# A four-layer graph network on one core: the second layer's adjacency product moves from VectorE to GpSimd, ahead of the transposes

## The reference

```
A (layer 0): e_ij = x_i.a_i + x_j.a_j, normalised over the graph, times adj plus adj, leaky relu,
             softmax over i, alpha @ x, sigmoid
B+C (layer 1): h = x Wp + bp; scores = leaky(s_src_i + s_dst_j) where adj > 0; attn = softmax over j
             weighted_adj = attn * adj;  h_gat = relu(layernorm(weighted_adj @ h))
             h_gin = (1+eps) h_gat + adj @ h_gat; z = relu(layernorm(h_gin W1 + b1)); relu(z W2 + b2 + h_gat)
D (layer 2): softmaxed adjacency (the same for all graphs), split in diagonal and rest: two products
E (layer 3): h = x W; attn = softmax(leaky(src_i + dst_j)) on edges and loops; elu(attn @ h)
```

## Time and profile before

| | us |
|---|---|
| median of 3 runs (1245.16 to 1245.55) | 1245.51 |
| the profiled execution's own time | 1249.84 |
| its span, first to last instruction | 1248.1 |
| busy: PE, DVE, ACT, POOL | 1111.1, 1096.2, 1020.0, 449.1 |
| share of the span | 89%, 88%, 82%, 36% |

### The profile page before, as it was taken

One profiled execution on the slowest core, in us unless ns is written; L12 is line 12 of the kernel. 1 busy time (PEld: TensorE's weight loads), 2 busy tenths in 40 slices (PEclk: granted clock), 3 DMA queues, 4 the chain that ended last, 5 costly groups with the idle time before them and its releaser, 6 DMA issues.

```text
span 1248.1 us, 29006 instructions
## 1 busy us (share of the span) xinstructions
PE 1111.1 (89%) x7632; PEld 903.1 (72%) x7632; DVE 1096.2 (88%) x4212; ACT 1020.0 (82%) x2582; POOL 449.1 (36%) x832
## 2 busy tenths in 40 slices
PE   6447889999999999999999999999999999999863
PEld 3235677888777777778877777777888777778753
DVE  5656789999999999999999999999999999998743
ACT  2244679999999888998999988889999999889764
POOL 4002324343334343444333334434443334443320
PEclk9667999999999999999999999999999999999986
DMA  3000001101100111111011011111101100110000
GB/s 64 17 26 9 27 26 35 35 26 34 34 22 20 34 34 34 34 34 34 25 34 33 10 32 34 34 34 34 34 25 34 34 21 21 34 35 26 18 9 17
DMA packets 59460, 35.94 MB, mean 29 GB/s; under 512 B 3873, under 2 KB 54817, under 8 KB 59425
## 3 DMA queue, kind: packets, MB, share of 16 engines
q1 hardware_dynamic: 59424, 35.54, 9.4%
HBM read 18.75 MB, written 8.39 MB: 22 GB/s over the span
## 4 chain that ended last, share of the span: by engine, by line
DVE 37%; PE 21%; issue 20%; POOL 9%; ACT 5%; DVEq 2%; DMA 1%; POOLq 0%; ACTq 0%; SPq 0%
PE ps L792 5%; DVE pTB L954 4%; DVE wE L928 3%; PE ps L761 3%; PE ps L777 3%; DVE vA L1027 3%; PE ps L667 3%; DVE wE L941 2%; DVE vA L1046 2%; POOL lnr_E L593 2%; POOL lnr_B L593 2%; DVE wB L928 2%; PE ps L660 2%; ACT xout L1213 2%; DVE wB L941 2%
## 5 line engine op out<-in xcount | busy, mean ns | idle before, releaser
L777 PE MATMUL ps<-hE,pTE 128*128 128x128 f32 x1024 | 136.4, 277 | 0.0
L708 PE MATMUL ps<-xsA,pA 128*128 128x128 f32 x1024 | 124.0, 280 | 7.4 <-ACT xsA L1268 7.4
L777 PE MATMUL ps<-hB,pTB 128*128 128x128 f32 x1024 | 126.3, 277 | 0.0
L777 PEld LDWEIGHTS ps<-hE,pTE 128*128 128x128 f32 x1024 | 125.0, 193 | 0.6 <-issue 0.4
L708 PEld LDWEIGHTS ps<-xsA,pA 128*128 128x128 f32 x1024 | 118.5, 194 | 9.2 <-ACT xsA L1268 8.3
L792 PE MATMUL ps<-gin_j,hgat 128*128 128x512 f32 x256 | 123.7, 607 | 0.0
L826 PE MATMUL ps<-att_j,xD 128*128 128x512 f32 x256 | 122.8, 603 | 0.0
L777 PEld LDWEIGHTS ps<-hB,pTB 128*128 128x128 f32 x1024 | 120.9, 194 | 0.1
L1258 ACT ACTIVATE pA<-vA,nmA,rirA 128x512 f32<-128x512 f32 x128 | 103.6, 816 | 16.7 <-issue 15.6
L928 DVE SCALAR_TENSOR_TENSOR wE<-ps,hE,y2E 128x512 f32<-128x512 f32 x128 | 94.7, 745 | 25.2 <-ACT y2E L1290 23.7
L1027 DVE CUSTOM_DVE_ANT_0 vA<-ps,adj_j 128x512 f32<-128x512 f32 x128 | 84.8, 682 | 17.7 <-PE ps L695 13.6
(11 more groups left out here) (237 smaller groups left out, 3115.2 us busy)
## 6 DMA issues: line engine op xcount, KB each, us to landing
xA<-in_x_dram SPq DMA_DIRECT2D x32, 256.0 KB, 2.8
xrA<-in_x_dram SPq DMA_DIRECT2D x32, 256.0 KB, 2.6
xrB<-xB SPq DMA_DIRECT2D x32, 256.0 KB, 2.3
out_dram<-xout SPq DMA_DIRECT2D x32, 256.0 KB, 2.2
adj_i<-in_adj_dram SPq DMA_DIRECT2D x1, 1024.0 KB, 5.3
a<-in_L_gnn_a_dram SPq DMA_DIRECT2D x2, 64.0 KB, 4.7
w_sb<-in_L_gnn_W_dram SPq DMA_DIRECT2D x2, 64.0 KB, 3.9
l2w<-in_L_gnn_W_dram SPq DMA_DIRECT2D x2, 64.0 KB, 3.4
```

What stands on the lines that cost most here:

```text
L708: last = mm(at("aggA")[:, i * P:(i + 1) * P], pA[:, j, i * P:(i + 1) * P], xsA[:, j], start=(j == 0), stop=(j == NT - 1))
L777: last = mm(at("agg" + n)[:, i * P:(i + 1) * P], att[n]["pT"][:, i, j], att[n]["h"][:, j, 0:P], start=(j == 0), stop=(j == NT - 1))
```

## The change

mult_B moves to GpSimd and ahead of the transposes: it multiplies the weights, as they come from the exponential, with adj_i (not transposed). PE transposes the product, and ScalarE copies the transposed tiles to pT, as it does for E. The exponential of B now writes into w in place, and the buffer that was p holds the product (paB). Beside that the steps' order on all five engines, the number of graphs by which each step lags, and the table of banks are written anew. No other step computes anything else than before. In the diff the first mult_B is the new one in GpSimd's program, the second the old one in VectorE's; the changed waits belong to weights_T (pT_B) and to leaky (L_B0).

```diff
+        paB = att[B]["p"]
+        att[B]["p"] = att[B]["w"]
         IN_BANK = [
-            [("aggA", 2), ("pairA0", 1), ("pE0", 5), ("aggE", 5)],
+            [("h012B", 2), ("h012E", 5), ("pairA2", 1), ("pB3", 2), ("aggA", 1), ("sumA", 0)],
...
+            def mult_B(i):
+                def step(g):
+                    pool.wait_ge(s["expB"], g.tile(i))
+                    if i == 0:
+                        pool.wait_ge(s["pTB"], NT * g.last)
+                    pool.tensor_tensor(paB[:, i], att[B]["p"][:, i], adj_i[:, i], ALU.mult).then_inc(s["paB"], 1)
...
-                READ_BY[f"pB{j}"] = ("paB", j, NT)
+                READ_BY[f"pB{j}"] = ("pcB", j, NT)
...
-                    pe.wait_ge(s["exp" + n], g.tile(i))
+                    pe.wait_ge(s["paB" if n == "B" else "expE"], g.tile(i))
...
-            agg_B0, agg_B1, agg_B2, agg_B3 = (aggregate("B", i, "paB") for i in range(NT))
+            agg_B0, agg_B1, agg_B2, agg_B3 = (aggregate("B", i, "pcB") for i in range(NT))
...
-                        dve.wait_ge(s["exp" + n], NT * g.last)
+                        dve.wait_ge(s["paB" if n == "B" else "expE"], NT * g.last)
...
-            def mult_B(i):
-                def step(g):
-                    dve.wait_ge(s["pTB"], g.tile(i))
-                    if i == 0:
-                        dve.wait_ge(s["aggB"], NT * g.last)
-                    v.tensor_tensor(att[B]["pT"][:, i], tiles(at(f"pB{i}")), adj_j[:, :, i * P:(i + 1) * P],
-                                    ALU.mult).then_inc(s["paB"], 1)
...
-            def copy_pE(i):
-                    act.wait_ge(s["pTE"], g.tile(i))
+            def copy_p(n, i):
+                    act.wait_ge(s["pT" + n], g.tile(i))
                     if i == 0:
-                        act.wait_ge(s["aggE"], NT * g.last)
-                    a.copy(att[E]["pT"][:, i].rearrange("p t d -> p (t d)"), at(f"pE{i}")).then_inc(s["pcE"], 1)
+                        act.wait_ge(s["agg" + n], NT * g.last)
+                    a.copy(att[n]["pT"][:, i].rearrange("p t d -> p (t d)"), at(f"p{n}{i}")).then_inc(s["pc" + n], 1)
...
-                t.run(mult_B0, 1)
-                t.run(bn_D, 3)
-                t.run(q_C, 2)
-                t.run(join_D, 3)
-                t.run(mult_B1, 1)
```

More of the change, by code:

```diff
@@ L600, in _ @@
             rstd_A, rstd_B, rstd_Z, rstd_C, rstd_D, rstd_E = (rstd(k) for k in "ABZCDE")
+            def mult_B(i):
[4 more added lines that the diff above has]
+                    pool.tensor_tensor(paB[:, i], att[B]["p"][:, i], adj_i[:, i], ALU.mult).then_inc(s["paB"], 1)
+                return step
+            mult_B0, mult_B1, mult_B2, mult_B3 = (mult_B(i) for i in range(NT))
             def power_A(g):
@@ L1177, in turn @@
                 t.run(M_B0, 1)
+                t.run(L_B2, 1)
                 t.run(M_B1, 1)
[L1179 to L1181 removed]
+                t.run(M_B2, 1)
+                t.run(v_A0, 0)
+                t.run(bn_Z, 2)
                 t.run(L_B3, 1)
[L1183 removed]
+                t.run(join_Z, 2)
+                t.run(v_A1, 0)
                 t.run(M_B3, 1)
[L1185 to L1202 removed]
+                t.run(v_A2, 0)
+                t.run(v_A3, 0)
+                t.run(max_A, 0)
+                t.run(lrelu_A0, 0)
+                t.run(offset_A, 0)
+                t.run(lrelu_A1, 0)
+                t.run(lrelu_A2, 0)
+                t.run(L_E0, 4)
+                t.run(L_E1, 4)
+                t.run(lrelu_A3, 0)
+                t.run(M_E0, 4)
+                t.run(M_E1, 4)
+                t.run(zz_B, 1)
+                t.run(recip_A, 0)
+                t.run(L_E2, 4)
+                t.run(M_E2, 4)
+                t.run(q_C, 2)
+                t.run(L_E3, 4)
+                t.run(bn_B, 1)
+                t.run(join_B, 1)
+                t.run(stats_B, 1)
+                t.run(M_E3, 4)
+                t.run(y_C, 2)
+                t.run(y_A, 0)
+                t.run(bn_A, 0)
+                t.run(join_A, 0)
             turns(dve, turn)
@@ L1417, in turn @@
+                t.run(norm_Z, 2)
+                t.run(exp_A0, 0)
+                t.run(exp_A1, 0)
+                t.run(copy_pB2, 1)
+                t.run(copy_zT, 2)
+                t.run(exp_A2, 0)
+                t.run(exp_A3, 0)
+                t.run(copy_pB3, 1)
+                t.run(scale_xA, 0)
                 t.run(norm_E, 5)
+                t.run(copy_xTD, 3)
             turns(act, turn)
```

209 lines of the change are left out of this document (88 added, 121 removed).

## The result

| | before | after |
|---|---|---|
| median of the runs, us | 1245.53 | 1353.41 (1349.13 to 1354.64) |
| ratio, 95% interval | | 1.0835 (1.0803 to 1.0867) |
| profiled execution: own time, span | 1249.84, 1248.1 | 1354.57, 1352.9 |
| first join_A ends, last join_A ends | 77.4, 1140.7 | 76.8, 1234.7 |
| mean period between them (31) | 34.30 | 37.35 |

The change costs 8.3%. Slower was the likelier side of the prediction, but the time lies 68 us above its range.

The account below looks back on a forecast made before the run. A loop of waits through several engines was taken as the bound: 32.9 us plus 1.95 of GpSimd holds gives 34.9 per graph; 178.3 + 31 x 34.9 = 1260.2, less 2.6, plus 1.3: 1259 us, range 1228 to 1285.

Parts of the forecast that it names:

- late load of xA: SyncE's load of the next graph's x: no wait was priced, its data being wanted some 7 us after release.
- steady period without it (31 graphs): Time per graph in the steady part: forecast 34.9 us, from 32.9 plus 1.95 of holds.
- what the filling saves: Between first and last A statistics joins: 31 periods less 6.5 us, taken unchanged from the kernel before.
- emptying: From last join_A to the end: 107.4 us kept, plus 1.3 for one product; up to 10 more possible.
- start: Up to the first graph's join of A statistics: 77.4 us, left as in the kernel before.
- The SP order ... costs nothing: SyncE's queue, both loads at the turn's start, xrB next: claimed free, xA's load released after scale_xA.
- The quarrel: GpSimd products and VectorE's two-SBUF-input steps exclude each other: mult_B2 and mult_B3 delay lrelu_A1 and lrelu_A2, 1.95 us together.
- the loop of 32.9: Aggregate A, VectorE's turn to lrelu_A3, exp_A3, copy_pB3, scale_xA, next aggregate A: 32.9 us, 34.9 with holds.
- the second loop: Shares the first loop's beginning, leaves VectorE at join_Z, then rstd_Z, norm_Z, four exp_A and copies on ScalarE: 34.0 us.
- the rivals: Harmless products, 1231 us, chance 0.24; one meeting, 1237 to 1247, 0.12; full VectorE relief, 1206, 0.05; late ScalarE, 1290, 0.09.
- The last one: ScalarE late with norm_C ahead of y2_B, so L_B0 starts late: with 1 us, period 35.9, median 1290; chance 0.09.
- lrelu_A keeps its 0.67 us: VectorE's lrelu_A unheld would show the forecast wrong; it expected two of four near 1.6 and 1.7 us.

Follow-up runs that it names:

- experiment 1: Changed kernel with only SyncE's order edited: the next graph's load of xA issued ahead of the store and the copy to xrB; 1296.14 us, ratio 1.0371.
- experiment 10: Kernel before with only SyncE's order taken from the changed kernel (load xA, load xrA, copy to xrB, store); 1247.09 us, ratio 0.9986.
- experiment 3: Changed kernel with the load of xA ahead and the GpSimd product cut to 4 of 512 columns, the rest filled by memset; 1242.07 us, ratio 0.9947.
- experiment 2: Changed kernel with the GpSimd product cut to 4 of 512 columns, the rest filled with ones by memset; 1313.41 us, ratio 1.0513.
- experiment 8: Kernel before with four products on GpSimd, each covering only 4 of 512 columns, and four copies on ScalarE; 1317.71 us, ratio 1.0555.
- experiment 9: Kernel before with only tile 3's product moved to GpSimd and its copy to ScalarE behind relu_E; 1257.60 us, ratio 1.0063.
- experiment 7: Kernel before with all four products on GpSimd and copies on ScalarE, other orders, lags and banks as before; 1332.11 us, ratio 1.0667.

## Why the prediction was wrong, point by point

Its formula was span = start + middle + end; with the forecast period and 1.3 us for one product in the last chain it gave 1261.5, and the span was 1352.9. The 91.4 us between are:

| term | forecast | changed kernel | off by | shown by |
|---|---|---|---|---|
| late load of xA | 0 | 57.5 | 57.5 | experiment 1 |
| steady period without it (31 graphs) | 34.9 | 35.4 | 15.5 | experiment 1 |
| what the filling saves | 6.5 saved | 3.0 lost | 9.5 | joins of experiment 1 |
| emptying | 108.7 | 118.2 | 9.5 | joins |
| start | 77.4 | 76.8 | -0.6 | joins |

- **The step that failed** is "The SP order ... costs nothing: the load of xA is released after scale_xA and its data is wanted by dots_A some 7 us later." Both halves were right by themselves. What I left out is what stands in front of the load in SyncE's list, and what that waits for: the copy to xrB, which waits for y_C, which the new VectorE order had put near the turn's end. The distance that I had put at 7 us was 8.0 (from 627.03 to 635.01, when dots_A could have begun). 6.7 us of waiting in the list and 2.9 of transfer don't fit into it, and 1.6 us are left over for dots_A to wait. Experiment 1 takes this wait away and nothing else, and experiment 10 shows that it needs both edits. The 57.5 us contain the long turns, which go with the load; at full clock it is 1.7 us a graph.
- **The quarrel**: size of the holds right, victims wrong, and so their price. I had 1.95 us on the second and third lrelu_A; it was 2.05 on max_A and offset_A. The product began at 617.81, when VectorE had just got to max_A, a step earlier than in my timing. I had let these 128x4 steps pass for free, because they are short. It makes a difference for the price: lrelu_A2 lies late in the order and would have delayed exp_A3 alone, the loop of 32.9; max_A and offset_A lie ahead of every exponential of A, and exp_A0 waits 1.47 us. So the hold came on top of the second loop: 33.8 (experiment 3) and 1.6 give 35.4. The prediction said 34.0 and 0.9.
- **The Trainium skill** (SBUF — State Buffer, "Who interferes with whom") had led me to the steps with two SBUF inputs. It holds for the small steps too: max_A is one, and was held for 1.0 us, and so is stats_B, by 0.6. The page also counts tensor_scalar among the operations that may take the shared ports with one input, and the trace agrees: offset_A was held by the product, and in experiment 2 still for 0.4 us by a fill that only writes, while max_A, which only needs the shared read port by that page, was not (162 ns).
- **The loop of 34.0 over norm_Z and ScalarE** was right (33.8 in experiment 3; the 0.2 us that rstd_Z was to wait for mult_B1 fall away there). Because of it, taking 2.44 us a graph off VectorE gains at best 0.7 of period (34.5 to 33.8), and filling and emptying take two thirds of that back: experiment 3 is only 8 us shorter than the kernel before, by spans.
- **The emptying** "could cost up to 10 us ... or nothing": it cost 10.8. It is 115 to 119 us in all kernels with the new lags and 107 to 111 in those with the old. I had carried none of it in the forecast.
- **Of the rivals** none was near. The last one, 1290 us with L_B0 late, had the right side; its mechanism (y2_B late) doesn't appear among the waits. What I named as a sign against the forecast, "lrelu_A keeps its 0.67 us", did occur.
- **Small slips**: VectorE's 860.4 us over 26 periods are 33.09 a graph and not 33.07, and PE's 856.7 are 32.95. Neither changes a forecast.
- **The range** took in the bounds of the terms that I had doubted, and nothing for the one that I had argued to zero.

Open: why the clock falls after some standstills and not after others; how much of the emptying is due to which lag; and whether an order exists in which the real products cost nothing. The best one that ran with all four products on GpSimd stays 1.7% above the kernel before.

## What to carry to other kernels

Of every transfer that is moved, read the list in front of it: the time at which it leaves is set by the latest wait of any entry ahead of it, and that wait may belong to a step which another part of the same change has moved. When work goes from one engine to a second, put the new instructions on the second engine's line between the two events that the loop goes through (here exp_B3 and scale_xA); if they all lie between, the period pays for them although that engine isn't full: 2.14 us for four copies of 0.47 us and a wait of 0.33 in experiment 8, 0.26 for one copy in experiment 9. And price a hold of the shared port by who waits behind the held step, not by how long the held step is.

## What the runs showed of the hardware

- A step of 128x4 with two SBUF inputs on VectorE went from 0.15 to 1.18 us beside a GpSimd product of 128x512, and a small tensor_scalar from 0.21 to 1.23. The longest hold of a step of 128x512 was about the same (M_B in experiment 7, 1.75 us in place of 0.68). So the hold doesn't shrink with the held step.
- A GpSimd fill of 128x508 (519 ns) held the small tensor_scalar for 0.4 us and left the small step with two inputs alone.
- A GpSimd product of 128x512 took 1.27 us as diag_D. mult_B, of the same shape, took 1.33 on average where it was put beside PSUM readers, and 1.46 in the changed kernel.
- After 1.4 to 2.2 us without work on PE the granted clock was 0.57 to 0.60 over the next 4 us in some turns, and 1.00 in others: 4 of 15 periods held such a stretch in the changed kernel, 10 of 15 in experiment 2, where the standstill was as long and the period shorter.
